# A decoder layer on one core: other order in the first FFN pair, and who makes Wo's low parts

## What is computed

```
x = layernorm(x + attn(x) @ w_o)                         # probs @ values, heads joined, then w_o
x = layernorm(x + softmax((x Wq' + bq)(ctx Wk' + bk)' / 32) @ ctx)
e = norm(x); w = where(e > 64, lut8, lut4)[codes]        # the kernel uses lut4
x = layernorm(x + x @ w' + bias)
```

## Time and profile before

| | us |
|---|---|
| median of three runs | 1260.17 (1259.99 to 1262.92) |
| the profiled execution | 1260.07 |
| its span, first to last instruction | 1258.0 |
| TensorE busy | 1229.6 (98% of the span) |
| VectorE, ScalarE, GpSimd busy | 860.1, 580.6, 617.7 |

### The profile page before, as it was taken

One profiled execution on the slowest core, in us unless ns is written; L12 is line 12 of the kernel. 1 busy time (PEld: TensorE's weight loads), 2 busy tenths in 40 slices (PEclk: granted clock), 3 DMA queues, 4 the chain that ended last, 5 costly groups with the idle time before them and its releaser, 6 DMA issues.

```text
span 1258.0 us, 25027 instructions
## 1 busy us (share of the span) xinstructions
PE 1229.6 (98%) x8134; PEld 1038.5 (83%) x8134; DVE 860.1 (68%) x2509; ACT 580.6 (46%) x1659; POOL 617.7 (49%) x522
## 2 busy tenths in 40 slices
PE   8999999999999999999999999999999999899997
PEld 6888889998788888888877887888888888678886
DVE  7999989565778888888776974253453635755654
ACT  5131213556777777777860222252342525532322
POOL 3512112458676776776750000454456554975552
PEclk9999999999999999999999999999999999999999
DMA  8154435364864344344443113317252444723221
GB/s 287 70 201 146 148 116 203 119 197 130 223 190 136 119 140 140 117 133 141 125 132 106 53 34 127 125 67 267 68 180 89 165 170 158 260 85 117 85 83 67
DMA packets 130833, 173.67 MB, mean 138 GB/s; under 512 B 36672, under 2 KB 91968, under 8 KB 130112
## 3 DMA queue, kind: packets, MB, share of 16 engines
q1 hardware_dynamic: 130752, 172.62, 42.2%
HBM read 115.94 MB, written 56.62 MB: 137 GB/s over the span
## 4 chain that ended last, share of the span: by engine, by line
PE 69%; POOL 14%; issue 10%; DMA 2%; DVE 2%; ACT 1%; SPq 1%; POOLq 0%; DVEq 0%; ACTq 0%
PE bank L773 14%; PE bank L775 13%; PE bank L774 13%; POOL prob L2165 10%; PE bank L859 5%; PE bank L1204 4%; PE bank L1206 4%; PE bank L1205 4%; PE bank L824 3%; PE bank L964 3%; POOL att_lo L2171 2%; PE bank L782 1%; PE bank L901 1%; PE bank L886 1%; PE bank L855 1%
## 5 line engine op out<-in xcount | busy, mean ns | idle before, releaser
L2165 POOL TENSOR_TENSOR prob<-prob,rinv 128x512 f32<-128x512 f32 x192 | 206.8, 1078 | 147.4 <-DVE rinv L1755 147.4
L1326 ACT ACTIVATE prob<-bank,nmax 128x256 f32<-128x256 f32 (+1 forms) x512 | 211.6, 429 | 76.0 <-DVE nmax L1747 70.0
L1747 DVE CUSTOM_DVE_ANT_0 bank<-bank,mask 128x256 f32<-128x256 f32 (+1 forms) x512 | 170.1, 385 | 38.0 <-PE bank L886 24.7
L901 PE MATMUL bank<-ident,prob 128*128 128x128 f32 x768 | 115.4, 273 | 1.3 <-ACT probT L1256 0.7
L901 PEld LDWEIGHTS bank<-ident,prob 128*128 128x128 f32 x768 | 94.5, 141 | 25.2 <-POOL prob L2165 2.4
L1326 ACT ACTIVATION_READ_ACCUMULATOR prob<-bank,nmax 128x1 f32 x512 | 109.7, 214 | 0.0
L964 PE MATMUL bank<-wo_hi,att_hi 128*128 128x512 f32 x256 | 104.3, 407 | 2.6 <-issue 2.6
L1902 DVE SCALAR_TENSOR_TENSOR k_lo<-bank,bA,k_hi 128x512 fp32r<-128x512 f32 x32 | 24.0, 751 | 120.9 <-ACT k_hi L1459 119.2
L886 PE MATMUL bank<-k,q 96*128 96x256 f32 (+1 forms) x512 | 104.2, 305 | 1.3 <-DMA vv<-v_scr 1.3
L964 PE MATMUL bank<-wo_hi,att_lo 128*128 128x512 f32 x256 | 101.3, 396 | 0.0
L964 PE MATMUL bank<-wo_lo,att_hi 128*128 128x512 f32 x256 | 101.2, 395 | 0.0
(11 more groups left out here) (221 smaller groups left out, 3247.0 us busy)
## 6 DMA issues: line engine op xcount, KB each, us to landing
q<-qk_scr SPq DMA_DIRECT2D x192, 128.0 KB, 2.4
x_st<-x_scr SPq DMA_DIRECT2D x32, 512.0 KB, 4.1
qk_scr<-rot SPq DMA_DIRECT2D x60, 256.0 KB, 2.6
xc_in<-x_cols SPq DMA_DIRECT2D x32, 256.0 KB, 4.7
y<-x SPq DMA_DIRECT2D x16, 512.0 KB, 3.6
x_scr<-y SPq DMA_DIRECT2D x16, 512.0 KB, 2.7
cx_in<-ctx_in SPq DMA_DIRECT2D x16, 512.0 KB, 4.9
x_scr<-x_st SPq DMA_DIRECT2D x16, 512.0 KB, 3.3
```

Source lines behind the costliest of these rows:

```text
L901: mm = nc.tensor.transpose(tb[:, at * P:(at + 1) * P], prob[:, k % 4, c:c + P], ident[:, :])
L1326: mm = nc.scalar.activation(prob[:, k % 4, i * keys:(i + 1) * keys], SBANK[pos][:, i * keys:(i + 1) * keys], ACT.Exp, bias=nmax[:, k % 4, ...
L1747: mm = nc.vector.tensor_tensor_reduce(part, part, mask[:, 2 * P - keys:2 * P], 1.0, BIGGEST, ALU.add, ALU.min, nmax[:, k % 4, i:i + 1])
L2165: nc.gpsimd.tensor_tensor(pr, pr, rinv[:, k % 4, 0:n].unsqueeze(2).to_broadcast([P, n, keys]), ALU.mult)\
```

## The change

- Wo's low parts are all made by GpSimd now, in halves of 512 columns (`wo_low`), at the steps of a new table `WO_LOW_STEPS`: blocks 2, 3, 0, 1 and 4 in batch 0, blocks 5, 6 and 7 in batch 1. The high parts of blocks 6 and 7 come two steps earlier. VectorE makes none.
- The projection's list takes blocks 0 to 4 for g = 0 and 1, then blocks 5 to 7, instead of six and two. This holds for all batches.
- `att_low` of pair 0 stands ahead of `scale_probs` of step 23, in all batches.
- FFN, SyncE: tile 2 of x2 is loaded ahead of unit T3, unit B22 after the store of the group's second tile, tile 3 after that.
- FFN, ScalarE: the high parts of pair 1's A11 and A12 go ahead of T4's high part, and both ahead of the norms.
- FFN, VectorE: T4's low part moves here from GpSimd. Pair 1's low parts and sums come after the addition of U3. In every pair, `part_low` of A22 comes after the addition and statistics of C11.
- FFN, GpSimd: `rstd2` of the last tile comes after the low part of S3.

```diff
--- before.py
+++ after.py
...
@@ -364,9 +364,11 @@
         RSTD_STEP = {16: (1, 0), 4: (2, 1)}
         NORM_STEP = {18: (1, 0), 6: (2, 1)}
         SPLIT_STEP = {22: (0, 0), 23: (0, 1), 1: (1, 2), 5: (1, 3)}
-        LOW_STEP = {23: (0, 0), 0: (1, 1), 2: (1, 2), 6: (1, 3)}
-        WO_STEPS = {(0, 12): 2, (0, 14): 3, (0, 18): 0, (0, 19): 1, (0, 20): 4, (0, 21): 5, (1, 5): 6, (1, 7): 7}
-        WO_EARLY = sum(age == 0 for age, _ in WO_STEPS)
+        LOW_STEP = {0: (1, 1), 2: (1, 2), 6: (1, 3)}
+        WO_STEPS = {(0, 12): 2, (0, 14): 3, (0, 18): 0, (0, 19): 1, (0, 20): 4, (0, 21): 5, (1, 3): 6, (1, 5): 7}
+        WO_LOW_STEPS = {(0, 13): ((2, 0), (2, 1)), (0, 15): ((3, 0), (3, 1)), (0, 19): ((0, 0), (0, 1)), (0, 20): ((1, 0), (1, 1)),
+                        (0, 21): ((4, 0), (4, 1)), (1, 3): ((5, 0), (5, 1)), (1, 5): ((6, 0), (6, 1)), (1, 7): ((7, 0),),
+                        (1, 8): ((7, 1),)}
         WO_TURN = {kt: i for i, kt in enumerate(WO_STEPS.values())}
         WO_FREE = {0: 3, 1: 3, 2: 5, 3: 5, 4: 9, 5: 9, 6: 11, 7: 11}
         WQ_HIGH_STEP, WQ_LOW_STEP = {9: 0, 12: 1}, {10: 0, 13: 1}
@@ -411,8 +413,8 @@
         X2PS = (bank[2], bank[3], bank[0], bank[1])
         U_BANK, P2_BANK, P5_BANK = (bank[6], bank[4]), bank[7], bank[5]
         U1_OUT, C11_OUT, U2_OUT, P5_OUT, U3_OUT, C12_OUT, C21_OUT = range(1, PARTS + 1)
-        BY_POOL = {F_B11: 0, F_B21: 2, F_T2: 4, F_T1: 6, F_T4: 8}
-        BY_DVE = {F_T3: 0, F_B22: 1}
+        BY_POOL = {F_B11: 0, F_B21: 2, F_T2: 4, F_T1: 6}
+        BY_DVE = {F_T3: 0, F_B22: 1, F_T4: 2}
 
         def f_source(i):
 
@@ -736,12 +738,14 @@
                 sp.dma_start(bias_bc[:, :], bias.rearrange("(a n) -> a n", a=1).to_broadcast([P, D])).then_inc(bias_ld, 16)
                 store_x2(g, 0)
                 sp.wait_ge(s2_done, GT * GROUPS)
-                for i in (F_T1, F_T3, F_B22):
-                    load_f(i)
+                load_f(F_T1)
+                sp.wait_ge(x2_stored[0], 16 * GROUPS)
+                load_x2(2)
+                load_f(F_T3)
                 store_x2(g, 1)
-                for t in range(2):
-                    sp.wait_ge(x2_stored[t], 16 * GROUPS)
-                    load_x2(2 + t)
+                load_f(F_B22)
+                sp.wait_ge(x2_stored[1], 16 * GROUPS)
+                load_x2(3)
                 sp.wait_ge(acc_done, LAST_ACC + 1)
                 load_f(F_T4)
                 for t in range(2, GT):
@@ -937,7 +941,7 @@
 
 
 
-            WO = [(g, kt, ps) for kts in (range(KT - 2), range(KT - 2, KT)) for g in (0, 1) for kt in kts for ps in range(3)]
+            WO = [(g, kt, ps) for kts in (range(KT - 3), range(KT - 3, KT)) for g in (0, 1) for kt in kts for ps in range(3)]
             WO += [(g, kt, ps) for g in (2, 3) for kt in range(KT) for ps in range(3)]
 
             def project(b, part):
@@ -955,10 +959,7 @@
                         else:
                             pe.wait_ge(att_lo_ready, 4 * b + kt // 2 + 1)
                     if g == 0 and ps == 0:
-                        if WO_TURN[kt] < WO_EARLY:
-                            pe.wait_ge(wo_lo_ready, WO_TURN[kt] + 1)
-                        else:
-                            pe.wait_ge(wo_lo2_ready, WO_TURN[kt] - WO_EARLY + 1)
+                        pe.wait_ge(wo_lo_ready, 2 * WO_TURN[kt] + 2)
                     lt = att_lo if ps == 2 else att_hi
                     rt = wo_lo if ps == 1 else wo_hi
                     mm = nc.tensor.matmul(o[:, :], lt[:, kt, st * P:(st + 1) * P], rt[:, kt, half * BANK:(half + 1) * BANK],
@@ -1580,9 +1581,12 @@
             f_unit_high(F_T3)
             act.wait_ge(acc_done, LAST_ACC + 1)
             f_unit_high(F_B22)
+            part_high(1, A11)
+            part_high(1, A12)
+            f_unit_high(F_T4)
             normalise2(GROUPS - 1, 2)
+            a21_out(1)
             normalise2(GROUPS - 1, 3)
-            f_unit_high(F_T4)
             def normalise3(n):
 
                 j = n % 2
@@ -1591,9 +1595,10 @@
                     .then_inc(y3_ready, 1)
 
             for q in range(1, TWOS):
-                part_high(q, A11)
-                part_high(q, A12)
-                a21_out(q)
+                if q > 1:
+                    part_high(q, A11)
+                    part_high(q, A12)
...
@@ -1819,10 +1824,6 @@
                         rope_item((k - 2) // 2)
                     if age == 1 and k == 3:
                         rope_item(11)
-                    if age == 1 and (age, k - 1) in WO_STEPS:
-                        kt = WO_STEPS[age, k - 1]
-                        dve.wait_ge(wo_hi_ready, WO_TURN[kt] + 1)
-                        low(wo_lo[:, kt, :], wo_in[:, kt, :], wo_hi[:, kt, :]).then_inc(wo_lo2_ready, 1)
                     if k in NORM_STEP and NORM_STEP[k][0] <= age:
                         normalise(b - NORM_STEP[k][0], NORM_STEP[k][1])
 
@@ -2077,18 +2078,17 @@
                 u = U_BANK[q % 2]
                 if q == 0:
                     stats_last(GROUPS - 1, GT - 1)
-                part_low(q, A22)
-
                 dve.wait_ge(x2b_ready, 2 * q + 1)
                 add_part(q, U1_OUT, A11, u, 0, 0)
 
                 dve.wait_ge(y3_part, PARTS * q + U1_OUT)
                 add_part(q, C11_OUT, A12, P2_BANK, 0, 0)
                 half_stats(q, C11_OUT, 0, 0)
+                part_low(q, A22)
                 if q == 0:
                     f_unit_low(F_T3)
                 add_part(q, U2_OUT, S2, u, 0, 1)
-                if q + 1 < TWOS:
+                if 0 < q < TWOS - 1:
                     part_low(q + 1, A11)
                     part_low(q + 1, A12)
                 if q == 0:
@@ -2096,11 +2096,17 @@
 
                 dve.wait_ge(x2b_ready, 2 * q + 2)
                 add_part(q, P5_OUT, S1, P5_BANK, 1, 1)
-                if q + 1 < TWOS:
+                if q == 0:
+                    f_unit_low(F_T4)
+                if 0 < q < TWOS - 1:
                     sums(q + 1)
 
                 dve.wait_ge(y3_part, PARTS * q + P5_OUT)
                 add_part(q, U3_OUT, S3, u, 1, 1)
+                if q == 0:
+                    part_low(1, A11)
+                    part_low(1, A12)
+                    sums(1)
                 half_stats(q, U3_OUT, 1, 1)
 
                 add_part(q, C12_OUT, S4, P5_BANK, 0, 1)
@@ -2176,22 +2182,29 @@
                 pool.wait_ge(wq_hi_ready, 2 * dt + half + 1)
                 nc.gpsimd.tensor_tensor(one(wq_lo), one(wq_in), one(wq_hi).bitcast(F32), ALU.subtract).then_inc(wq_lo_ready, 1)
 
+            def wo_low(kt, half):
+
+                cols = slice(half * BANK, (half + 1) * BANK)
+                pool.wait_ge(wo_hi_ready, WO_TURN[kt] + 1)
+                nc.gpsimd.tensor_tensor(wo_lo[:, kt, cols], wo_in[:, kt, cols], wo_hi[:, kt, cols].bitcast(F32), ALU.subtract)\
+                    .then_inc(wo_lo_ready, 1)
+
             def stage2_batch(b, age):
                 for k in range(SUB):
                     if k in RSTD_STEP and RSTD_STEP[k][0] <= age:
                         rstd1(b - RSTD_STEP[k][0], RSTD_STEP[k][1])
+                    if k == SUB - 1:
+                        att_low(b, 0)
                     scale_probs(b, k)
                     if k in LOW_STEP and LOW_STEP[k][0] <= age:
                         att_low(b - LOW_STEP[k][0], LOW_STEP[k][1])
                     if age == 0 and k >= 7 and k % 2 == 1:
                         rope_low(item_pair((k - 3) // 2))
-                    if age == 0 and (0, k - 1) in WO_STEPS:
-                        kt = WO_STEPS[0, k - 1]
-                        pool.wait_ge(wo_hi_ready, WO_TURN[kt] + 1)
-                        nc.gpsimd.tensor_tensor(wo_lo[:, kt, :], wo_in[:, kt, :], wo_hi[:, kt, :].bitcast(F32), ALU.subtract)\
-                            .then_inc(wo_lo_ready, 1)
                     if age == 1 and k == 4:
                         rope_low(item_pair(11))
+                    if age < 2 and (age, k) in WO_LOW_STEPS:
+                        for kt, half in WO_LOW_STEPS[age, k]:
+                            wo_low(kt, half)
                     if age and k in WQ_LOW_STEP:
                         wq_low(b - 1, WQ_LOW_STEP[k])
 
@@ -2303,12 +2316,11 @@
             f_unit_low(F_T1, (0,))
             sum_low(0, S2)
             f_unit_low(F_T1, (1,))
-            rstd2(GROUPS - 1, GT - 1)
             sum_low(0, S1)
             add_bias(1)
             sum_low(0, S3)
+            rstd2(GROUPS - 1, GT - 1)
             sum_low(0, S4)
-            f_unit_low(F_T4)
             for q in range(TWOS):
                 if q:
                     rstd3(2 * q - 1)
```

More of the change, by code:

```diff
@@ L275, in decoder_layer @@
         t_step = sem("t_step")
-        wo_ld, wo_hi_ready, wo_lo_ready, wo_lo2_ready = (
-            sems("wo_ld", KT // 2), sem("wo_hi_ready"), sem("wo_lo_ready"), sem("wo_lo2_ready"))
+        wo_ld, wo_hi_ready, wo_lo_ready = (
+            sems("wo_ld", KT // 2), sem("wo_hi_ready"), sem("wo_lo_ready"))
```

(7 more changed lines are left out.)

## The result

The changed kernel is slower: **1281.61 us** (median of 4 runs, 1280.28 to 1282.74) against 1261.08 us for the kernel before (4 runs, 1259.99 to 1262.92). The ratio is 1.0148, 95% interval 1.0126 to 1.0171 (the two medians alone give 1.0163). The forecast was 1256.6, with 1259.4 as its upper end. The profiled execution took 1282.56 us (its span 1280.8).

The account below looks back on a forecast made before the run. TensorE, busy 47.80 of 48 us in steady batches, was taken as the bound, so only its idle time could be won: 0.9 + 2.5 = 3.4 us off 1260.07 gives 1256.6 us, range 1253.2 to 1259.4.

Parts of the forecast that it names:

- Both places: Batch 1 of the attention, some 0.9 us won, and the FFN's first two pairs, 2.5 us won.
- rival 2: Clock falls again at waits in batch 1 or the FFN's start, 1.7 us each: 1258.3, about 1260 if both; chance 0.16.
- After step 12 both versions run without a wait: Batch 1 of the attention: no TensorE waits follow step 12, so the gain there stays some 0.9 us.
- take turns: FFN start: when VectorE subtracts two SBUF tensors, it and GpSimd alternate, the waiting one going next; S3 then starts at 1094.0.
- Rival 1: FFN start: turns fall otherwise; by bare durations 8.3 us won, hence 1250.9, or a smaller form, 1255.0; chance 0.22.
- rival 3: Later FFN pairs: VectorE's low part of A22 comes late; one microsecond in each of six pairs gives 1262.6; chance 0.04.
- place 1: Batch 1 of the attention, around 306 us: GpSimd's queue lets step 12 begin at 330.4 instead of 331.4, some 0.9 us won.
- In batches 2 to 7 ...: 0: Attention, batches 2 to 7: att_lo moves within GpSimd's slack and Wo's new block division changes no count, so gain 0.

Follow-up runs that it names:

- the code put back in place: Changed kernel with two idle semaphore increments on VectorE just ahead of its loop over batches 2 to 7: 1258.49 us, ratio 0.9970.
- the four starts: Positions where VectorE's loop begins in its program, across the kernels run: 959 (bad), 960 (good), 961 (good) and 1073 (bad).
- the best one: Changed kernel with two idle VectorE increments and GpSimd's low parts of S3 and S4 ahead of tile 1's bias and last row's statistics: 1256.30 us, ratio 0.9944.
- the one with S3 first: Changed kernel with two idle VectorE increments and GpSimd's low part of S3 ahead of tile 1's bias: 1260.25 us, ratio 0.9983.
- those with one or two increments alone: Changed kernel with only one or two idle semaphore increments ahead of VectorE's loop: 1258.55 us (one), 1258.49 us (two).

## Why the prediction was wrong

**Both places came out as worked out, as far as the working went.** In batch 1 the first Wo matmul starts at 306.01 without idle; the late half of block 7's low part ends at 329.21 (forecast 329.0); TensorE waits for it and goes on at 329.26:

```profile
327.95 1.26 POOL L2189 TENSOR_TENSOR wo_lo<-wo_in,wo_hi 128x512 fp32r<-128x512 f32 x1
```

```profile
329.26 0.50 PE L965 MATMUL bank<-wo_hi,att_hi 128*128 128x512 f32 x1 [1.41 <-POOL wo_lo L2189]
```

```profile
331.00:333.50 2.50, 2.50 (x10) 2.01 (x10) 1.77 (x7) 1.40 (x4) 2.17 (x3) 0.50 1.01 166
```

Step 12 came 0.94 us earlier, measured from the batch's start; the forecast was 0.9. The window shows rival 2 at this place: the clock is at 1.2 GHz from 330.51 for 3.41 us. By step 13 the 0.94 had become 0.43 us of loss, and by step 12 of batch 2, where TensorE had waited another 0.74 us for V's loads, 1.1. So "After step 12 both versions run without a wait" didn't hold, and this term was 2.0 us off.

In the FFN VectorE and GpSimd take turns, as the earlier trace rows had it. The three f_lo of VectorE (T3, B22, T4; alone 2.28) and GpSimd's work beside them (the bias alone 2.39, a low part 1.29, the power 0.55):

```profile
1110.63 3.26 DVE L1615 TENSOR_TENSOR f_lo<-f_in,f_hi 128x2048 fp32r<-128x2048 f32 x1
...
1114.41 3.88 DVE L1615 TENSOR_TENSOR f_lo<-f_in,f_hi 128x2048 fp32r<-128x2048 f32 x1
...
1118.81 2.76 DVE L1615 TENSOR_TENSOR f_lo<-f_in,f_hi 128x2048 fp32r<-128x2048 f32 x1
```

```profile
1111.70 4.43 POOL L2281 TENSOR_TENSOR x_st<-x_st,bias_bc 128x1024 f32<-128x1024 f32 x1
1116.10 3.32 POOL L2286 TENSOR_TENSOR x2T_lo<-x_sum,x2T_hi 128x512 fp32r<-128x512 f32 x1
1119.38 2.59 POOL L2299 TENSOR_TENSOR rv<-rv,neg_half 128x1 f32<-128x1 f32 x1
```

```profile
1119.47 0.79 PE L1205 MATMUL bank<-f_hi,x2T_hi 128*128 128x512 f32 x1 [3.67 <-POOL x2T_lo L2286]
```

With the 25.75 us taken off by which the FFN began later, S3 started at 1093.7 (forecast 1094.0), S4 at 1097.9 (1098.3), A22 at 1100.7 (1101.1) and S2 of pair 1 at 1109.7 (1110.2). The gain is 3.0 us, the forecast 2.5. Rival 1's bare durations are wrong, rival 3 too: from pair 1 on S2 of one pair follows S2 of the one before by the same 20.84 us as before (20.04 for the last). Rival 2 happened at both places (half clock from 330.51 and from 1118.99, 3.41 us each), but its 1.7 us were paid only at the first: at S3 the slow matmuls ended at 1123.69, and the low part that S4 waits for at 1123.60.

**The step that failed** is in place 1: "VectorE loses two wo_lo of its own here; it isn't waited for, so that is worth nothing", with "In batches 2 to 7 ...: 0". Time was counted for what leaves VectorE, but not its place in the program. Those instructions stood ahead of a loop that fitted its blocks with one instruction to spare on that side, start 961 with the border at 960, and without them the loop costs 24.5 us more. In the sum, -3.4 should have been -3.0 (FFN), +1.1 (batch 1 with its clock) and +24.5 (code): 22.6 us, where the spans differ by 22.8. With the code put back in place, the ratio is 0.9970, and the forecast's was 1256.6 / 1260.07 = 0.9972. That the two agree so closely is in part luck: the interval is more than ten times as wide as their difference, and with the same attention one kernel won 0.7 us there and another lost 1.6. As a risk the stall was foreseeable: the trace of before shows no instruction packet between 401 and 701 us, so that its loops live on code that stays, and the two built programs show by how much the loop moves. That a border lay just there only the runs showed.

The Trainium skill (Runtime: NRT & Kernel Launch, "Instruction fetch mechanics") says that a taken branch whose target isn't in the present window forces a fetch before execution goes on. By that rule the traces agree: 5.2 to 5.9 us a branch. It gives the refill as blocks of 16 KiB (256 instructions); the packets here have 8 KB and the four starts fit 128 instructions, and the measurement decides.

## What to carry to other kernels

Where an engine runs a loop, treat every instruction added or removed ahead of it, on that engine, as a change to the loop: compare the start of its body in the two built programs and look for instruction packets in the stretch of the loop, before costing the edit at nothing. If they appear, first move the loop by one or two idle instructions, and only then judge the rest. And where two engines take turns, look at what goes first in a queue and not only at what each instruction takes alone: here one low part moved gained nothing, two moved gained 2 us.

## What the runs showed of the chip that was not expected

- A backward branch cost VectorE 5.2 to 5.9 us when its body touched four blocks and began one instruction ahead of a border, 3.3 to 3.4 us when it began 15 ahead, and nothing (0.49 us to the first instruction, waiting for scores) with three. The first two fetches stand 2.6 us apart (406.82 and 409.43), which fits two in a row for the first case; that this is their order is read from these times, not tested.
- The same waits don't always slow the clock. In batch 1 TensorE waited 1.7 and 1.4 us at the same two matmuls in seven of these kernels; the clock then fell in three, the changed kernel (330.51), the best one (330.57) and the one with S3 first (331.40), and didn't in four, among them those with one or two increments alone. A fall is 3.41 us at half speed, 1.7 us, and where it comes is part of what one kernel's runs differ by (1256.2 to 1263.0 in ten). What decides it stays open.
